# A gather ring of 28 slots in place of 49 in a four-layer graph network kernel

## The reference

```
x = layernorm(x + x @ W(edge_weight at src, dst))
cnt[n, r] = edges of type r into n;  inv_deg = 1 / max(cnt[dst, type], 1)
X = x
for l in range(4):
    h   = einsum('ni,rio->rno', X, W[l])                # 4 products per node, 256 wide
    msg = h[type, src] * inv_deg
    out = segment_sum(msg, dst) + X @ root[l] + bias[l]
    X   = elu(layernorm(out) * gamma[l] + beta[l]) + X
x = layernorm(x + X)
```

## Time and profile before

| | us |
|---|---|
| median of three runs (2712.81 to 2717.09) | 2713.06 |
| the profiled execution's own time | 2710.93 |
| its span, first to last instruction | 2709.2 |
| PE busy | 2199.1 (81%) |
| DVE busy | 1557.3 (57%) |
| POOL busy | 1512.8 (56%) |
| ACT busy | 371.0 (14%) |

### The profile page before, as it was taken

The page is one execution under the profiler, slowest core; times in us unless marked ns, Lnnn a source line. Parts: engine busy times, 40 slices in busy tenths (PEclk is TensorE's granted clock), DMA queues, the critical chain, the costliest instruction groups (busy, mean ns, idle before and its releaser), DMA issues.

```text
span 2709.2 us, 45161 instructions
## 1 busy us (share of the span) xinstructions
PE 2199.1 (81%) x7889; PEld 1327.8 (49%) x7890; DVE 1557.3 (57%) x5264; ACT 371.0 (14%) x765; POOL 1512.8 (56%) x1591
## 2 busy tenths in 40 slices
PE   4668966778788889888898898988889968777776
PEld 2435444666344555434455563344455534445554
DVE  7988079997344566434455663344556623446676
ACT  2553400331000111100011110000111100000000
POOL 1000051003777777377777764777777567777773
PEclk9878965999678999867789996578899966777788
DMA  5000340001344444333444442334444343334342
GB/s 160 0 0 8 148 141 16 0 0 41 105 120 129 136 151 144 96 105 113 121 129 144 144 146 84 105 113 128 129 144 152 119 146 105 104 105 119 105 120 63
DMA packets 103215, 280.43 MB, mean 104 GB/s; under 512 B 27676, under 2 KB 39050, under 8 KB 102798
## 3 DMA queue, kind: packets, MB, share of 16 engines
q0 software_dynamic: 75264, 205.62, 26.4%
q10 hardware_dynamic: 18224, 62.59, 6.2%
q1 hardware_dynamic: 9566, 10.42, 1.3%
HBM read 219.61 MB, written 58.91 MB: 103 GB/s over the span
## 4 chain that ended last, share of the span: by engine, by line
PE 48%; issue 13%; DVE 13%; POOL 11%; DMA 9%; DVEq 3%; ACT 1%; POOLq 1%; ACTq 0%; SPq 0%
PE acc L465 26%; POOL ring L275 11%; DMA ring<-h_rows,idx 9%; PE hp L372 7%; PE pw L372 7%; PE acc L454 3%; DVE S L883 3%; PE acc L457 2%; PE pw L348 1%; DVE hot_s L856 1%; DVE ring L753 1%; DVE hot_n L856 1%; POOLq L181 1%; ACT XT L501 1%; PE tr L361 1%
## 5 line engine op out<-in xcount | busy, mean ns | idle before, releaser
L275 POOL DMA_INDIRECT ring<-h_rows,idx x1568 | 1505.2, 960 | 1156.1 <-issue 880.9
L465 PE MATMUL acc<-ring,S 128*128 x3712 | 1227.0, 471 | 196.8 <-SPq L228 144.7
L906 DVE TENSOR_SCALAR S<-iota,ecol 128x128 f32<-128x128 f32 x1856 | 610.4, 366 | 860.2 <-PE acc L465 739.2
L465 PEld LDWEIGHTS acc<-ring,S 128*128 128x128 f32 x3712 | 749.4, 223 | 666.0 <-issue 590.6
L372 PE MATMUL hp<-wts,XT 128*128 (+1 forms) x416 | 212.3, 658 | 22.4 <-ACT XT L501 22.4
L372 PE MATMUL pw<-wts,XT 128*128 (+1 forms) x384 | 196.9, 661 | 20.3 <-ACT XT L501 20.3
L454 PE MATMUL acc<-wts,XT 128*128 (+1 forms) x400 | 124.7, 441 | 62.3 <-issue 62.3
L564 ACT ACTIVATE work<-work 128x256 f32<-128x256 f32 x100 | 41.7, 417 | 908.8 <-DVE work L935 899.9
L856 DVE TENSOR_TENSOR hot_s<-iota,place 128x400 bf16<-128x400 f32 x196 | 111.4, 569 | 89.2 <-PE acc L415 84.9
L372 PEld LDWEIGHTS hp<-wts,XT 128*128 128x128 f32 x416 | 83.6, 212 | 120.4 <-issue 120.4
L454 PEld LDWEIGHTS acc<-wts,XT 128*128 128x128 f32 x400 | 83.5, 217 | 119.7 <-issue 109.9
(11 more groups left out here) (206 smaller groups left out, 1365.5 us busy)
## 6 DMA issues: line engine op xcount, KB each, us to landing
h_rows<-hst ACTq DMA_DIRECT2D x100, 512.0 KB, 3.1
ring<-h_rows,idx POOLq DMA_INDIRECT x1568, 2.8
wts<-weights SPq DMA_DIRECT2D x32, 128.0 KB, 3.1
x_rows<-X ACTq DMA_DIRECT2D x1, 3200.0 KB, 10.2
wts<-x_rows ACTq DMA_DIRECT2D x1, 3200.0 KB, 12.4
X<-x SPq DMA_DIRECT2D x1, 3072.0 KB
out<-X ACTq DMA_DIRECT2D x2, 1024.0 KB
wts<-roots SPq DMA_DIRECT2D x8, 128.0 KB, 2.9
```

Of the source, the lines that this page charges most:

```text
L275: pool.indirect_dma_start(ring[:, k, :], None, h_gather, bass.IndirectOffsetOnAxis(ap=idx[:, g * J + j:g * J + j + 1], axis=0)).then_inc(l ...
L465: nc.tensor.matmul(accs[t % 2][:, 0:D], S[:, at * J + j, :], ring[:, bass.ds((c + j) % SLOTS, 1), :].rearrange("p a d -> p (a d)"), start= ...
L906: v.tensor_scalar(S[:, at * J + j, :], iota[:, t * P:(t + 1) * P], dst_c[:, bass.ds(c + j, 1)], inv_c[:, bass.ds(c + j, 1)], ALU.is_equal, ...
```

## The change

The ring is used with 28 slots in place of 49. The allocation stays at 49 slots (ROOM), since other arrays of the preparation lie in it. All that depends on SLOTS follows: columns go to slot c modulo 28, there are 28 landing semaphores, SP's inner loop goes over 28 slots and runs CYC = 14 times a layer in place of 8, and the ring's wait of group g asks for the visits to columns below 4g - 13 in place of 4g - 34. No instruction of PE, DVE, ACT or POOL is added, removed or moved.

```
-SLOTS = 49
+SLOTS = 28
+ROOM = 49
 CYC = NG * J // SLOTS
 assert CYC * SLOTS == NG * J
...
-        ring = sb("ring", [P, SLOTS, D])
+        ring = sb("ring", [P, ROOM, D])
```

## The result

The changed kernel takes 2744.52 us, the median of four runs from 2741.38 to 2747.37, against 2713.42 for the kernel before. The ratio is 1.0111 with a 95% interval from 1.0094 to 1.0129, so 30 us slower, between 25 and 35 (the two medians are 31 us apart). The forecast was 2738.5, which is 25 us slower.

What follows compares the result with a forecast made beforehand. POOL's gather pace was taken to bound the layers. 25.1 + 0.8 - 0.3 = 25.6 us on the profiled 2710.93 gave 2736.5; that execution lying 2.1 us under the median, 2738.5 was forecast, from 2735 to 2743, with half-shares of rivals 2733 to 2747.

Steps and rivals of the forecast that it cites:

- The bound: In the layers, POOL issues gathers at its own pace of about 1.25 us each, and PE follows it.
- Part 1, the head start: Layer 0: 16 gathers ahead in place of 36; twenty steps cost 25.1 us, a later restart 0.8 us.
- Part 2, the room: Inside the layers: 13 columns of look-ahead suffice and POOL doesn't stop; value 0, bounds -1 and +24 us.
- The margin of 2.3 us: Group 72 of layer 1, the closest in layers 0 to 2: slack of 3.2 us less 0.9 for release.
- rival 2: Inside the layers: 24 tight groups cost POOL 1 us each, 2762 us; a third of that 2747; chance 12%.
- Part 3, SP's loop: SP's loop edge comes 14 times a layer in place of 8, but is hidden; value 0, bounds 0 and 14 us.
- rival 4: SP's relays show in the time, up to 14 us, 2752 us; chance 4%.
- The 0.3 us of the early stretch: Before layer 0's aggregation: 20 fewer gathers beside DVE's one-hot work give back 0.3 us at most.
- 1 (PE sets the end): Layer 0's end is set by PE, so the head start is worth nothing, 2713 us; chance 6%, half for 2726.
- 5 (no change): The change doesn't do what it says, the held groups still allow 36 gathers ahead, 2713 us; chance 1%.
- 3 (the early pace of 1.62 us): Gathers moved into layer 0 keep the early pace, 32.4 us in place of 25.1, so 2746 us; chance 5%.
- The weighing of the rule on the shared port pair: DVE's 2-port modes could hold up moved gathers beside making S; judged unlikely, 80 gathers at twice the DVE work.

Runs made afterwards that it cites:

- hold16: Kernel before with its 49 slots, but POOL waits ahead of group 4 for three visits, so layer 0's head start is 16 gathers; 2740.9 us, ratio 1.0108.
- hold4: Kernel before with its 49 slots, but POOL waits ahead of group 1 in each layer, so layer 0's head start is 4 gathers; 2765.01 us, ratio 1.0208.
- second profile: The 28-slot kernel run once more unchanged, 2740.79 us; its pair is the kernel before run once more, 2713.4 us.
- look13_late: Kernel before with 49 slots and head start of 36, but groups from 24 on wait for visits below column 4g - 13; 2715.26 us, ratio 1.0013.
- look9_late: Kernel before with 49 slots and head start of 36, but groups from 24 on wait for visits below column 4g - 9; 2749.25 us, ratio 1.0143.
- sp7_ring28: 28-slot kernel with SP's inner loop over two turns of the ring, its edge 7 times a layer in place of 14; 2737.73 us, ratio 1.0101.
- head28_ring28: 28-slot kernel without waits for slots never used, so 28 gathers ahead in place of 16; 2731.4 us, ratio 1.0067.
- ring28_warm: 28-slot kernel with two more PE products ahead of the last tile's turn in each of three layers; 2735.93 us, ratio 1.0082.

## Why the prediction was right, and where it was off

**The bound.** POOL's own pace bounds the layers, as read from the earlier trace rows. One reading on the way was loose: of the 880.9 us put down to "issue", 351.84 lie ahead of the first gather and about 98 in the three turns; the other 430 or so are the time between two gathers. Taking gathers out of layer 0's head start cost a step each in hold16 and hold4, with 49 slots. PE's 81% was no bound: in the first 50 us of layer 0 it was busier after the change with 41 instructions fewer.

**Part 1, the head start.** Expected 25.1 + 0.8 us, restart at 650.6, last gather at 1121. The changed kernel has 650.80 and 1122.23, in the second profile 1121.33. The shift is 26.5 and 26.8 us, so the term of 25.9 was up to 1 us small. That PE had caught up by the end of tile 0, and so hid nothing, is borne out by this shift going through to the end of the program.

**Part 2, the room.** Right that 13 columns suffice in layers 0 to 2, and that the one stop would be in layer 3's last group: 1.0 us there, where up to 1.5 was expected. The value of 0 is slightly small, by look13_late 3.5 us with 1 to 6 as its interval. The margin of 2.3 us that I worked out from ends of visits was right: with 5 us less, POOL stopped in every layer. The same comparison on the changed kernel's own trace gives 2.7 us of slack at the least in layers 0 to 2 once the held gathers run (group 5 of layer 0), then 3.0 (group 57 of layer 0) and 3.1 (group 70 of layer 2). In look9_late a stopped gather starts 0.8 us after the visit that it needs. What I had priced wrongly, in rival 2 as in the expectations, is what an overdrawn margin costs. I took it as a late start once or 1 us a time; it came back at six or seven groups of each layer, 1 to 3 us each. My reading is that PE, which follows POOL, is late by as much at the next tile; that isn't shown apart.

**Part 3, SP's loop.** Hidden: rival 4's full 14 us is excluded by sp7_ring28, and the layers of the second pair of profiles take no longer with the more frequent edge.

**The sum.** 25.6 us were expected and 30 measured, 25 to 35 by the interval. The forecast lies at the interval's lower end, so a gap of 4 to 5 us is likely but hardly more than the noise; the second pair of profiles has 27.4 us and sp7_ring28, with the same slots, 27. The mechanism was right; that the sum came so close is in part luck, since the prediction had no term for the turns. I had taken them as fixed at 33 to 34 us. In all profiles they lie between 32.2 and 36.1 us and go mostly with PE's last products, which take 1.4 to 2.8 us more where the clock is lower. In the six turns of the changed kernel none had the products at 3.67 us, in the six of the kernel before three had. Whether that is the ring or chance is open: hold4 speaks against the head start as the cause, and sp7_ring28 and head28_ring28 each have one turn at 3.67 us with 28 slots. ring28_warm shows only that the time is there to be had. The 1 to 6 us of look13_late may be the same thing or a cost of the room.

Two slips of the working changed little. The 0.3 us of the early stretch was valued at nothing and then taken off in the sum. And half of rival 2's 24 us would be 2750, outside of the range that was said to take it in; the range holds a third of it.

**The rivals.** 1 (PE sets the end) and 5 (no change) fell with the result. 3 (the early pace of 1.62 us) would have put layer 0's last gather at 1129; it is at 1122. 2 and 4 are bounded as above. The weighing of the rule on the shared port pair, from the Trainium skill (SBUF — State Buffer, "Who interferes with whom"), stands: 376 gathers beside the making of S kept a step of 1.257 us.

## What to carry to other kernels

When a queue has one pace whatever its neighbours do, count how much of it is done before its stretch begins: each item that a ring's depth lets run ahead in an idle phase is worth one full step, and that can be the whole value of the depth. In the steady part, depth is worth next to nothing (here 1 to 6 us for 21 of 34 columns) down to the point where it no longer covers the consumer's stretch without a release, and a great deal below it, so work out the slack group by group before cutting. A wait's formula that is safe in the steady part can be needlessly strict for slots that were never used; look there for free head start.

## What the runs showed of the hardware that was not expected

- Eight identical products at the end of a layer took 3.67, 5.37 or 6.42 us, at granted clocks of 1.00, 0.72 and 0.62 over the stretch, after the same wait of 2.05 us. The full level is 2.4 GHz and the low one 1.2. With two products of 0.9 us each put into the wait, they took 3.67 us in all six turns of two kernels; without them, in 14 of the 36 turns of the other profiles.
- POOL's indirect gathers of 128 rows have a step of 1.25 us in the layers with DVE busy for 34 or for 68 us of 100, and of 1.62 us in the early stretch beside DVE's line 856. All of the difference is in the instruction's own length, 1.31 us on the mean in place of 0.95. It seems to depend on which instruction DVE runs and not on how busy it is. In the trace of the kernel before, 894 gathers beside nothing but line 906 (tensor_scalar) have a mean step of 1.251 us and 157 beside no DVE instruction 1.250, but 45 beside lines 932 to 936, two scalar_tensor_tensor among them, 1.306, and the 36 beside the tensor_tensor of line 856 1.62. The slower early pace came again in every kernel. No run took DVE's work away from it, so the cause isn't shown.
